# First attention of a two-layer block: loads of the stacked q and k walk the 8 features outermost instead of the 3 repeats

## The chip, the cores and the metric

The kernel runs on one core of a Trainium2 chip. The metric is the device time of one execution in microseconds (us). The profile comes from one execution of the same program.

## The reference, cut to what matters

The model is a block of two layers over an input of 16 batches of 128 rows and 256 columns. Its first step, and the only one that the change touches, is a cross attention with 16 heads of 8 features:

```
q = split_heads(einsum('bsf,of->bso', layernorm(x)^T, Wq) + bq)     # 16 heads, head size 8
k = split_heads(einsum('bsf,of->bso', ctx^T, Wk) + bk)
v = split_heads(einsum('bsf,of->bso', ctx^T, Wv) + bv)
attn = softmax(einsum('bhqd,bhkd->bhqk', q, k) / sqrt(128))         # 256 x 256 for each of 16 heads and 16 batches
out = einsum('bhqk,bhkd->bhqd', attn, v);  x = x + tanh(g) * (out Wo + bo)^T
```

After it come a layer of 64 experts, an mLSTM, and a second block with attention and four experts.

## The kernel before, in words

The code is written for the five engines one by one, with semaphores between them and every order fixed by hand.

The float32 q and k of the first attention are each split into three bf16 parts. A score needs all nine products of a part of q with a part of k, so nine blocks of 8 features are stacked on the contraction axis: 72 rows (`TERM_ROWS`) of 16 heads x 256 positions, 8 KB a row. Rows 72 to 74 (`MAX_ROWS`) hold the three parts of the negative row maximum against rows of ones in k, so that a second product gives the scores with the maximum already taken off. Tiles `qs` and `ks` hold one batch each, in a ring of four (`A_RING`).

- In a first stage (to about 70 us) q and k of all batches are computed, split and stored to DRAM as `a_q_parts` and `a_k_parts`, each [batch, 3 parts, 128, 256] in bf16 (`store_parts`, L161). Row p of the 128 is feature d = p // 16 of head p % 16, so that one feature of all heads is one contiguous run of 8 KB. ScalarE can write `parts` of pair i only when the stores of pair i - 3 have landed.
- `stack(b)` (L164) fills the tiles of batch b from DRAM with six DMAs of 192 KB. For t = 0, 1, 2 it loads rows 24t to 24t + 23: in `qs` three repeats of part t of q (L175), in `ks` the three parts of k once (L176). `stack(0)` is issued after the third `store_parts`; `stack(1)` to `stack(3)` after the last; then four loads of kept weights (below); and `stack(b + 4)` once the last exponentials' product of batch b is done.
- TensorE runs over heads: `score_max` (L262, 72 rows) puts the scores of a head in a bank and VectorE takes their maximum (L481), 28 heads ahead (`AHEAD`) of `exponentials` (L290, 75 rows), whose bank ScalarE turns into exponentials (L398); `times_v` (L304), `normalise` (L314), `to_features` (L323) and `residual` (L328) finish the batch. When a batch's 16 maxima are there, TensorE turns them into rows (L272), ScalarE and GpSimd split them in three (L385 to L536), and SyncE loads them into rows 72 to 74 of `qs` with three DMAs of 8 KB (`max_rows`, L204). `exponentials(b, 0)` waits for these three.
- Beside this, weights of the last block are split in two parts ("kept" work): at each `max_rows` SyncE stores the split of two units (L190, four DMAs of 256 KB) and loads two new ones (L184, two of 256 KB), which wait for those stores. GpSimd does the rounding.

All DMAs go through SyncE's one queue, so they are issued in this order: ..., `max_rows(b)`, stores, loads, `stack(b + 3)`, `max_rows(b + 1)`, ...

Of the kernel before, what the change touches and what calls it, by code (L numbers as in the profile page):

```python
# [23 lines left out]
DMA = 16  # L24
# [47 lines left out]
HEADS, HD = 16, 8  # L72
POS = D
# [34 lines left out]
def kept_units(k):  # L108

    io, units = k.io, []  # L110
    for h in range(RH):
        units.append((io["b_wqk"][h], [k.qk_parts[h, i] for i in range(2)]))
    for g in range(RH // GROUP):
        for half in range(2):
            cols = slice(half * KEPT, (half + 1) * KEPT)
            units.append((io["b_wv"][g][:, cols], [k.v_parts[g, i][:, cols] for i in range(2)]))
    for h in range(0, RH, 2):
        units.append((io["b_wo"][h:h + 2].rearrange("h p n -> p h n"), [k.o_parts[h:h + 2, i].rearrange("h p n -> p h n") for i in range(2)]))
    return units


def kept_places(k, u, shape):

    first = (u % KEPT_SLOTS) * 2 * KEPT
    whole, high = (k.columns[:, :, :].rearrange("p k t -> p (k t)")[:, at:at + KEPT] for at in (first, first + KEPT))
    return [t if len(shape) == 2 else t.rearrange("p (h n) -> p h n", h=shape[1]) for t in (whole, high)]


def kept_of(b):

    return range(KEPT_EACH * b, min(KEPT_EACH * (b + 1), 2 * RH))
# [9 lines left out]
def layer0_sp(k, m, s, ring):  # L141

    sp, io = k.nc.sync, k.io

    def load_inputs(chunk):
        b = slice(chunk * CHUNK, (chunk + 1) * CHUNK)
        sp.dma_start(k.resid[:, b, :], io["x"][b, :, :].rearrange("b p n -> p b n")).then_inc(k.x_in[chunk], DMA)
        sp.dma_start(k.ctx[:, b, :], io["ctx"][b, :, :].rearrange("b p n -> p b n")).then_inc(k.ctx_in[chunk], DMA)

    load_inputs(0)  # L150
    sp.dma_start(k.gates[:, :], io["gates"]).then_inc(k.gates_in, DMA)
    for dst, name in ((m.wqT, "a_wqT"), (m.wkT, "a_wkT"), (m.wvT, "a_wvT"), (m.woT, "a_woT"), (m.bias, "a_bias")):
        sp.dma_start(dst[:, :], io[name]).then_inc(s.weights_in, DMA)
    for chunk in range(1, NCHUNK):
        load_inputs(chunk)

    def store_parts(i):
        for n, (name, ready) in enumerate((("q", s.q_low), ("k", s.k_low))):
            sp.wait_ge(ready, i + 1)
            for j in range(2):  # L160
                sp.dma_start(io[f"a_{name}_parts"][2 * i + j].rearrange("t p n -> p t n"),  # L161
                             m.parts[i % A_SLOTS][:, n, :, j * POS:(j + 1) * POS]).then_inc(ring[f"{name}_out"][i % A_SLOTS], DMA)

    def stack(b):  # L164
        r, i = b % A_RING, b // 2
        flat = lambda t, first, count: t[first * HD:(first + count) * HD, :, :].rearrange("p h n -> p (h n)")
        parts_of = lambda n: io[f"a_{n}_parts"][b].rearrange("t (d h) n -> t d (h n)", d=HD)
        sp.wait_ge(ring["q_out"][i % A_SLOTS], 2 * DMA * (i // A_SLOTS + 1))
        sp.wait_ge(ring["k_out"][i % A_SLOTS], 2 * DMA * (i // A_SLOTS + 1))
        if b < A_RING:  # L170
            sp.wait_ge(s.k_ones, b + 1)
        else:
            sp.wait_ge(s.exp_scores, (b - A_RING + 1) * HEADS)
        for t in range(3):
            sp.dma_start(flat(m.qs[r], 3 * t, 3), parts_of("q")[t].unsqueeze(0).broadcast_to([3, HD, HEADS * POS])).then_inc(ring["stack_in"][r], DMA)  # L175
            sp.dma_start(flat(m.ks[r], 3 * t, 3), parts_of("k")).then_inc(ring["stack_in"][r], DMA)  # L176

    units = kept_units(k)

    def load_kept(u):  # L180
        r = u % KEPT_SLOTS
        if u >= KEPT_SLOTS:
            sp.wait_ge(ring["kept_out"][r], 2 * DMA * (u // KEPT_SLOTS))
        sp.dma_start(kept_places(k, u, units[u][0].shape)[0], units[u][0]).then_inc(ring["kept_in"][r], DMA)  # L184

    def store_kept(u):
        low, high = kept_places(k, u, units[u][0].shape)
        sp.wait_ge(s.kept_low, u + 1)
        for dst, src in zip(units[u][1], (high, low)):
            sp.dma_start(dst, src).then_inc(ring["kept_out"][u % KEPT_SLOTS], DMA)  # L190

    def kept(b):

        if b:
            for u in kept_of(b - 1):
                store_kept(u)
            for u in kept_of(b + 1):
                load_kept(u)

    def max_rows(b):  # L200
        sp.wait_ge(s.max_split, b + 1)
        for part in range(MAX_ROWS):
            row = TERM_ROWS + part
            sp.dma_start(m.qs[b % A_RING][row:row + 1, :, :].rearrange("o h (q n) -> o (h q) n", q=2),  # L204
                         m.mparts[b % 2][:, part, :]).then_inc(ring["max_in"][b % A_RING], DMA)
        kept(b)

    for i in range(1, NB // 2 + 1):
        store_parts(i - 1)
        if i == 3:  # L210
            stack(0)
    for b in range(1, A_RING):
        stack(b)
    for u in range(KEPT_SLOTS):
        load_kept(u)
    for i in range(AHEAD):
        if i >= 2 and (i - 2) % HEADS == HEADS - 1:
            max_rows((i - 2) // HEADS)
    for n in range(A_STEPS):
        for h in range(2):  # L220
            i = 2 * n + h + AHEAD - 2
            if i % HEADS == HEADS - 1 and i // HEADS < NB:
                max_rows(i // HEADS)
        if n % A_PAIRS == A_PAIRS - 1 and n // A_PAIRS + A_RING < NB:
            stack(n // A_PAIRS + A_RING)
    for u in kept_of(NB - 1):
        store_kept(u)
    for r in range(KEPT_SLOTS):
        sp.wait_ge(ring["kept_out"][r], 2 * DMA * (2 * RH // KEPT_SLOTS))
# [2084 lines left out]
```

## Time and profile before

| what | us |
|---|---|
| time, median of 3 runs | 1835.76 (1823.01 to 1838.44) |
| the profiled execution's own time | 1829.41 |
| its span in the trace | 1828.1 |
| first attention within it | about 0 to 391 |
| TensorE busy | 1633.9 (89%) |
| VectorE busy | 1103.7 (60%) |
| ScalarE busy | 1007.5 (55%) |
| GpSimd busy | 609.9 (33%) |

Busy time is the sum over the instructions of an engine. The chain of waits goes back from the last instruction, at each step to what released it. "PEclk" is the clock granted to TensorE, as a share of 2.4 GHz: 1.00 is 2.4 GHz and 0.50 is 1.2 GHz. In a list of instructions, [3.92 <-DMA x] means that the engine stood idle for 3.92 us before this one until DMA x landed. "SPq" stands for DMAs issued by SyncE: their time is that of the issue, not of the transfer.

### The profile page before, as it was taken

To read this page: it belongs to the slowest core of one execution; us is meant where nothing else is said; L and a number is where in the kernel's file an instruction comes from. 1 tells how busy PE (TensorE), PEld (TensorE's weight loads), DVE (VectorE), ACT (ScalarE), POOL (GpSimd) and SP (SyncE) were. 2 spreads that over 40 slices of the span, in tenths; PEclk is the share of its full clock that TensorE was granted. 3 is DMA by queue.
4 is the path that set the end of the run, shared out by engine and by line. 5 is a ranking of instruction groups with operands and counts; after the bars stand their busy time and mean duration, and the time that the engine had idled before them with its cause. 6 is when DMAs were issued, how large, how long until landed. Compare 5 with 4: busy or idle time off the path is not lost.

```text
span 1828.1 us, 30253 instructions
## 1 busy us (share of the span) xinstructions
PE 1633.9 (89%) x10996; PEld 1279.5 (70%) x10996; DVE 1103.7 (60%) x2052; ACT 1007.5 (55%) x2050; POOL 609.9 (33%) x495
## 2 busy tenths in 40 slices
PE   4368889878999999999998695899999999999898
PEld 2135455436888888888886342688888888888687
DVE  6456677637854445544446457676777777667454
ACT  4246667664443334433333664776777877776443
POOL 5222223212443533333332001454455455444000
PEclk9568888889999999999998787899999999999799
DMA  5634545335344334344330001435434334332310
GB/s 158 156 101 155 152 159 170 120 125 130 104 105 114 109 99 113 101 111 112 107 96 4 8 4 35 147 110 170 137 110 139 122 111 139 127 113 71 78 47 24
DMA packets 110980, 196.15 MB, mean 107 GB/s; under 512 B 16664, under 2 KB 59484, under 8 KB 108016
## 3 DMA queue, kind: packets, MB, share of 16 engines
q1 hardware_dynamic: 110832, 194.21, 35.9%
q8 instruction: 89, 1.46, 0.3%
q14 instruction: 59, 0.48, 0.1%
HBM read 167.64 MB, written 25.73 MB: 106 GB/s over the span
## 4 chain that ended last, share of the span: by engine, by line
PE 69%; DMA 8%; DVE 7%; ACT 5%; issue 5%; SPq 3%; POOL 3%; POOLq 0%; ACTq 0%; DVEq 0%
PE bank L67 16%; PE bank L69 16%; PE bank L68 16%; DMA a_qs<-a_mparts 6%; PE bank L1790 3%; PE bank L1758 3%; PE bank L304 2%; PE bank L290 2%; PE bank L262 2%; PE bank L1780 1%; POOL e_hidden L1008 1%; PE bank L1290 1%; PE bank L1289 1%; SPq L204 1%; PE bank L1300 1%
## 5 line engine op out<-in xcount | busy, mean ns | idle before, releaser
L1008 POOL TENSOR_TENSOR e_hidden<-e_gated,e_comb_wide 128x512 f32<-128x512 f32 x132 | 211.3, 1600 | 347.0 <-DVE e_gated L973 331.1
L848 ACT CAST e_hidden_hi<-e_hidden 128x512 fp32r<-128x512 f32 x132 | 82.0, 622 | 321.2 <-POOL e_hidden L1008 321.2
L481 DVE TENSOR_REDUCE a_negmax<-bank 128x2 f32<-128x512 f32 x256 | 166.7, 685 | 104.9 <-PE bank L262 103.5
L966 DVE TENSOR_TENSOR e_hidden_lo<-e_hidden,e_hidden_hi 128x512 fp32r<-128x512 f32 x132 | 98.2, 744 | 211.5 <-ACT e_hidden_hi L848 211.5
L69 PE MATMUL bank<-e_x_hi,e_weights_lo 128*128 128x512 f32 (+1 forms) x528 | 209.3, 396 | 0.0
L67 PE MATMUL bank<-e_x_hi,e_weights_hi 128*128 128x512 f32 (+1 forms) x528 | 208.4, 395 | 0.7 <-ACT e_comb_rows L808 0.7
L68 PE MATMUL bank<-e_x_lo,e_weights_hi 128*128 128x512 f32 (+1 forms) x528 | 208.3, 395 | 0.0
L1869 ACT ACTIVATE b_turned<-bank,b_swap_bias 64x512 f32<-64x512 f32 x256 | 174.9, 683 | 43.1 <-PE bank L69 39.3
L398 ACT ACTIVATE a_exp<-bank 128x512 f32<-128x512 f32 x256 | 144.3, 596 | 71.9 <-PE bank L290 66.0
L2018 POOL TENSOR_TENSOR b_turned<-b_turned,b_rope_q 128x512 f32<-128x512 f32 x64 | 82.8, 1294 | 258.8 <-ACT b_turned L1869 258.8
L69 PE MATMUL bank<-e_weights_hi,e_hidden_lo 128*128 128x256 f32 (+1 forms) x528 | 149.0, 282 | 0.0
L67 PE MATMUL bank<-e_weights_hi,e_hidden_hi 128*128 128x256 f32 (+1 forms) x528 | 147.8, 280 | 0.5 <-DVE e_hidden_lo L966 0.5
L68 PE MATMUL bank<-e_weights_lo,e_hidden_hi 128*128 128x256 f32 (+1 forms) x528 | 148.0, 280 | 0.0
L290 PE MATMUL bank<-a_qs,a_ks 75*128 75x256 bf16 x512 | 108.0, 298 | 41.1 <-DMA a_qs<-a_mparts 40.2
L262 PE MATMUL bank<-a_ks,a_qs 72*128 72x256 bf16 x512 | 114.5, 312 | 33.0 <-DMA a_ks<-a_k_parts 13.7
L1968 DVE TENSOR_TENSOR b_straight<-b_straight,b_turned 128x512 f32<-128x512 f32 x128 | 141.2, 1141 | 0.0
L973 DVE TENSOR_TENSOR e_gated<-e_silu,bank 128x512 f32<-128x512 f32 x132 | 90.5, 686 | 56.6 <-PE bank L69 44.1
L1935 DVE SCALAR_TENSOR_TENSOR b_straight<-bank,b_head_bias,b_rope_q 128x512 f32<-128x512 f32 x64 | 48.0, 749 | 111.2 <-ACT b_turned L1869 111.1
L69 PEld LDWEIGHTS bank<-e_x_hi,e_weights_lo 128*128 128x128 f32 (+1 forms) x528 | 98.7, 187 | 22.8
L67 PEld LDWEIGHTS bank<-e_x_hi,e_weights_hi 128*128 128x128 f32 (+1 forms) x528 | 99.2, 188 | 19.7 <-ACT e_comb_rows L808 1.1
L68 PEld LDWEIGHTS bank<-e_x_lo,e_weights_hi 128*128 128x128 f32 (+1 forms) x528 | 98.7, 187 | 18.8
L67 PE MATMUL bank<-b_x_hi,b_qk_hi 128*128 128x512 f32 x256 | 102.5, 401 | 4.8 <-DVE b_x_lo L1927 3.4
(327 smaller groups left out, 4156.6 us busy)
## 6 DMA issues: line engine op xcount, KB each, us to landing
e_comb_wide<-e_combT SPq DMA_DIRECT2D x130, 256.0 KB, 4.0
e_raw<-in_e_weights SPq DMA_DIRECT2D x64, 384.0 KB, 4.6
b_qk_hi<-b_qk_parts SPq DMA_DIRECT2D x64, 256.0 KB, 2.7
b_qk_lo<-b_qk_parts SPq DMA_DIRECT2D x64, 256.0 KB, 3.0
a_qs<-a_q_parts SPq DMA_DIRECT2D x48, 192.0 KB
a_ks<-a_k_parts SPq DMA_DIRECT2D x48, 192.0 KB
b_qk_parts<-columns SPq DMA_DIRECT2D x32, 256.0 KB, 3.6
b_vw_hi<-b_v_parts SPq DMA_DIRECT2D x16, 512.0 KB, 3.9
```

Of the source, the lines that this page charges most:

```text
L67: pe.matmul(out, w_hi, x_hi, start=start, stop=False, skip_group_check=True)
L68: pe.matmul(out, w_hi, x_lo, start=False, stop=False, skip_group_check=True)
L69: return pe.matmul(out, w_lo, x_hi, start=False, stop=stop, skip_group_check=True)
L262: last = pe.matmul(bank[:, qb * POS:(qb + 1) * POS], m.qs[r][0:TERM_ROWS, h, qb * P:(qb + 1) * P], m.ks[r][0:TERM_ROWS, h, :], start=True, ...
L290: last = pe.matmul(bank[:, kb * POS:(kb + 1) * POS], m.ks[r][0:ROWS, h, kb * P:(kb + 1) * P], m.qs[r][0:ROWS, h, :], start=True, stop=True)
L398: act.activation(m.expo[at % A_EXPS][:, :, :].rearrange("p k q -> p (k q)"), banks[2 + h % 2][:, :], ACT.Exp, scale=float(1 / np.sqrt(np.f ...
L481: dve.tensor_reduce(m.negmax[b % 2][:, h, :], banks[h % 2][:, :].rearrange("p (q n) -> p q n", q=2), AX.X, ALU.max, negate=True).then_inc( ...
L966: dve.tensor_tensor(lo[0:rows, :], m.hidden[at % 2][0:rows, :], hi[0:rows, :].bitcast(F32), ALU.subtract).then_inc(s.hidden_lo)
L973: dve.tensor_tensor(m.gated[i][0:rows, :], m.silu[i][0:rows, :], banks[2 * i + 1][0:rows, :], ALU.mult).then_inc(s.gated)
L1008: pool.tensor_tensor(m.hidden[i][0:rows, :], m.gated[i][0:rows, :], m.comb_wide[u % E_RING][0:rows, chunk * BANK:(chunk + 1) * BANK], ALU. ...
L1869: last = act.activation(w.turned[i][dst:dst + half, which, :], banks[bank][src:src + half, :], ACT.Identity, bias=m.swap_bias[dst:dst + ha ...
L1968: dve.tensor_tensor(w.straight[n % 2][:, which, :], w.straight[n % 2][:, which, :], w.turned[n % 2][:, which, :], ALU.add).then_inc(s.rotated)
```

## The change

Both access patterns of the source change their outermost dimension. Before, a load of q walks 3 repeats (step 0), then 8 features, and one of k walks 3 parts, then 8 features. After, both walk 8 features first, and inside each the 3 repeats or the 3 parts. The destination, 24 rows of 8 KB, is the same, so row 24t + 8r + d of before becomes row 24t + 3d + r in both tiles; the products of a score are the same, added in another order. The bytes moved, the number of DMAs, their order in the queue and all waits stay.

```diff
     def stack(b):
         r, i = b % A_RING, b // 2
         flat = lambda t, first, count: t[first * HD:(first + count) * HD, :, :].rearrange("p h n -> p (h n)")
-        parts_of = lambda n: io[f"a_{n}_parts"][b].rearrange("t (d h) n -> t d (h n)", d=HD)
+        parts_of = lambda n: io[f"a_{n}_parts"][b].rearrange("t (d h) n -> d t (h n)", d=HD)
...
         for t in range(3):
-            sp.dma_start(flat(m.qs[r], 3 * t, 3), parts_of("q")[t].unsqueeze(0).broadcast_to([3, HD, HEADS * POS])).then_inc(ring["stack_in"][r], DMA)
+            sp.dma_start(flat(m.qs[r], 3 * t, 3), parts_of("q")[:, t:t + 1].broadcast_to([HD, 3, HEADS * POS])).then_inc(ring["stack_in"][r], DMA)
             sp.dma_start(flat(m.ks[r], 3 * t, 3), parts_of("k")).then_inc(ring["stack_in"][r], DMA)
```

## Rows read from the trace of the kernel before

**Rows 1.** The page: shares of the chain that ended last, by engine

```profile
PE 69%; DMA 8%; DVE 7%; ACT 5%; issue 5%; SPq 3%; POOL 3%; POOLq 0%; ACTq 0%; DVEq 0%
```

**Rows 2.** Chain in order of time, 40 to 400 us: start, us, what

```profile
46.09 11.69 DMA a_q_parts<-a_parts
...
100.96 13.33 DMA a_qs<-a_mparts
...
243.67 10.17 DMA a_qs<-a_mparts
...
315.45 10.26 DMA a_qs<-a_mparts
```

**Rows 3.** Waits of PE, 60 to 395 us: total, times, longest

```profile
PE bank L290 <- DMA a_qs<-a_mparts: 40.2, 12, 13.4
...
PE bank L262 <- DMA a_ks<-a_k_parts: 13.7, 1, 13.7
```

**Rows 4.** Busy time by stretch; DMA share is of 16 engines

```profile
core 0: us, PE busy (x) PEld busy (x) DVE busy (x) ACT busy (x) POOL busy (x), PEclk, DMA share, GB/s
102.00:108.00 6.00, 0.00 (x0) 0.00 (x0) 0.00 (x0) 0.00 (x0) 0.00 (x0) 0.50 0.20 80
250.00:252.00 2.00, 0.00 (x0) 0.00 (x0) 1.05 (x4) 0.13 (x1) 0.00 (x0) 0.84 0.19 78
187.00:191.00 4.00, 4.00 (x42) 2.38 (x40) 3.38 (x8) 3.44 (x10) 2.18 (x5) 1.00 0.69 150
74.00:84.00 10.00, 3.75 (x13) 0.77 (x12) 4.73 (x8) 0.00 (x0) 0.00 (x0) 0.50 0.73 144
133.29:365.35 232.06, 205.14 (x1831) 117.53 (x1829) 155.63 (x325) 151.20 (x313) 61.84 (x91) 0.85 0.49 151
217.60:227.60 10.00, 9.23 (x58) 4.49 (x59) 3.85 (x7) 4.37 (x9) 1.53 (x4) 0.51 0.51 129
230.85:244.63 13.78, 13.78 (x145) 8.28 (x142) 11.78 (x25) 11.54 (x24) 3.68 (x8) 1.00 0.56 169
```

**Rows 5.** DMA issues of SyncE in order of time, one batch

```profile
238.33 0.77 SPq L175 DMA_DIRECT2D a_qs<-a_q_parts  x1
...
242.43 1.84 SPq L204 DMA_DIRECT2D a_qs<-a_mparts  x3
244.31 2.12 SPq L190 DMA_DIRECT2D b_qk_parts<-columns  x4
```

**Rows 6.** TensorE in order of time: one clean batch, then a wait

```profile
225.75 1.86 PE L304 MATMUL bank<-a_exp,a_vaug 128*9 128x256 f32 x16
...
230.85 0.44 PE L323 MATMUL bank<-ident,a_outq 128*128 128x128 f32 x2
...
240.34 1.05 PE L304 MATMUL bank<-a_exp,a_vaug 128*9 128x256 f32 x16
...
244.63 0.44 PE L323 MATMUL bank<-ident,a_outq 128*128 128x128 f32 x2
...
253.89 0.61 PE L290 MATMUL bank<-a_qs,a_ks 75*128 75x256 bf16 x2 [3.92 <-DMA a_qs<-a_mparts]
```

**Rows 7.** TensorE, transposes of the maxima, batches 2 and 15

```profile
133.29 0.28 PE L272 MATMUL bank<-ident,a_negmax 128*32 128x128 f32 x1
...
365.35 0.28 PE L272 MATMUL bank<-ident,a_negmax 128*32 128x128 f32 x1
```

**Rows 8.** SyncE issues, 68 to 98 us

```profile
70.94 0.71 SPq L175 DMA_DIRECT2D a_qs<-a_q_parts  x1
...
83.09 3.54 SPq L176 DMA_DIRECT2D a_ks<-a_k_parts  x1
86.69 10.99 SPq L184 DMA_DIRECT2D columns<-in_b_wqk  x4
```

**Rows 9.** Issues that fill q and k stacks, L175 and L176: ns min/median/max

```profile
L175 SPq DMA_DIRECT2D a_qs<-a_q_parts x48: 697/746/2021, 41.5 to 330.9; - x48
...
L176 SPq DMA_DIRECT2D a_ks<-a_k_parts x48: 403/445/3545, 42.4 to 331.6; - x48
```

**Rows 10.** Loads of the maxima (L204), from issue to landing

```profile
DMA to landing us min/median/max: 1.8/2.9/13.3
```

## The prediction, written before the changed kernel was run

> **What bounds the kernel now.** I first read the shares of the chain that ended last: TensorE has 69%, but a DMA share of 8% stands beside it [rows 1], some 146 us of 1828, and the change is about DMAs. The chain in order of time shows where they lie. In the first attention it goes again and again through one transfer, the load of the maxima into rows 72 to 74 of `qs`, with 10.17 and 10.26 us from issue to landing for 8 KB; the first takes 13.33 us; and earlier there is one of 11.69 us, a store of q parts [rows 2]. Alone, such a load of maxima takes as little as 1.8 us [rows 10]. So it isn't its own size that makes it late, but what lies ahead of it on the DMA engines. TensorE stands still for it 40.2 us in 12 waits, and once 13.7 us for a stack [rows 3].
>
> What lies ahead is seen in the DMA share by stretch. Just before a wait ends, the share is 0.19 to 0.20 of 16 engines at 78 to 80 GB/s, in two stretches 150 us apart [rows 4]: that is 3 engines at some 26 GB/s each, and 13 empty ones. Nothing but stack loads runs there, and 3 is the outermost count of the q load. Earlier in a stack the share is 0.69 to 0.73 at 144 to 150 GB/s [rows 4], 11 or 12 engines. I read this so: a k load is spread over 12 engines, a q load over 3, and engines 0 to 2 carry both. A q load is 24 rows of 8 KB, 196.6 KB, so three take 590 KB / 78 GB/s = 7.6 us; the k loads another 590 KB / 150 = 3.9 us; together 11.5 us. The case of one batch agrees: the stack's issue begins at 238.33, the maxima are issued from 242.43 [rows 5] and land at 243.67 + 10.17 = 253.84 [rows 2], 15.5 us after the stack began, and TensorE goes on at 253.89 after 3.92 us of idling [rows 6].
>
> The wait costs twice. After it the granted clock is at 0.51 for 10 us [rows 4], the lower of the two levels, 1.2 GHz, and a `times_v` group takes 1.86 us in place of 1.05 at 2.4 GHz [rows 6].
>
> **The change, part by part.**
>
> *Spread of the loads.* The outermost count of both sources becomes 8. I take 8 engines for all six loads, at 26 GB/s each 208 GB/s: 1.18 MB a stack in 5.7 us. The other bound is the rate at which 11 or 12 engines did these loads, 150 GB/s, which is no better per engine than 13: 7.9 us. I take 7.5, nearer to the measured rate of the same rows. Against 11.5 to 12 now.
>
> The Trainium skill, DMA: Bandwidth & Descriptors, in the section on why a DMA increments its semaphore by 16, says that a DMA uses the largest number of engines up to 16 that divides the outermost sizes of both sides; for 3 against 24 rows that is 3, for 8 against 24 it is 8, and the rows with 3 engines agree. The same rule speaks against half of the change: the k loads lose engines (12 to 8). The SBUF page (SBUF — State Buffer, Door 1) says that 24 neighbouring partitions reach only 6 of 16 ports of 27.2 GB/s; an estimate from it is 163 GB/s whatever the number of engines, so 7.2 us a stack, and k would lose nothing. The 144 to 150 GB/s of 12 engines agree with such a ceiling.
>
> *The 13 batches in the middle.* From the maxima's transpose of batch 2 (133.29) to that of batch 15 (365.35) [rows 7] there are 13 periods in 232.06 us, 17.85 each, with a mean clock of 0.85 [rows 4]. One without a wait and at full clock lasted 244.63 - 230.85 = 13.78 us, with TensorE busy for all of it [rows 6, 4]; it is the price of a batch when TensorE is the bound. Is the wait gone? In the case above the stack begins at 238.33, late, since SyncE's loads of kept weights ahead of it wait for stores that themselves lie behind the last stack. The transfer starts at about 239.1, ends 7.5 us later at 246.6, and the maxima, in the queue since 244.3 [rows 5], land some 1.5 us after, at about 248. TensorE needs them at 253.89 - 3.92 = 249.97 [rows 6]. With 7.9 us it is still 1.6 us in time. And since the stores ahead also land sooner, the next stack is issued sooner. So I take all waits as gone: 13 x (17.85 - 13.78) = 52.9 us, of which the idle time itself is 40.2 - 13.4 = 26.8 us [rows 3] and the rest lower clock. Lower bound: some waits of a microsecond stay and keep the clock down now and then; with half of the periods clean it is 30 us. Upper bound 55.
>
> *The start.* The store of q parts at 46.09 lands at 57.78 [rows 2], behind `stack(0)`, whose issue begins at 41.5 [rows 9]. With transfers from 42.5 to 50, store and landing come at about 52: 5.5 us earlier (3 to 7). Then `stack(1)` to `stack(3)` are issued from 70.94 on [rows 8], now 65.4. The 18 loads take 22.5 us from 66.2, so to 88.7; the four kept loads behind them, 1 MB, have half on the same eight engines, 0.52 MB / 208 GB/s = 2.5 us; the first maxima follow with 1.5: 92.7 to 93.2. Before, they landed at 100.96 + 13.33 = 114.3 [rows 2]. That is 21 us with the 5.5 in it. TensorE's wait of 13.7 us for the second stack [rows 3] mostly goes inside this: the stack lands at some 75, and the maxima are computed well before 93. At 5.7 us a stack the start gives 27 us, at 9 it gives 16.
>
> *What it costs.* The k load has one dimension more, as the q load has now: its issue may take 0.75 us in place of 0.45 [rows 9], 0.9 us a stack. Behind it in SyncE's queue stand the maxima of the next batch; 0.9 us fits in the 1.6 to 2 us left above. Before the first maxima it is 9 x 0.3 = 2.7 us, covered by transfers that run until 88.7, while the issues of SyncE that now take 3.54 and 10.99 us [rows 8] should shorten. Without that cover it would cost 2.7 us. The order of rows costs TensorE nothing: same shapes, same number. Everything behind 391 us is untouched.
>
> **Sum.** 52.9 + 21 = 74 us off the profiled execution's 1829.4: 1755. The median of the runs shown lies 6.4 us above that execution, so the same sum gives 1762 there. I forecast 1758, between the two.
>
> **Rivals.**
>
> *The stack gains half or less.* Eight engines on few partitions could get in each other's way: a stack takes 10 to 11 us. For it: 12 engines did no better than 150 GB/s. Against: 3 did 78. Then a stack started at 238.3 lets the maxima land at about 251, a wait of 1 us in many batches with the clock down after each; I put 2 us a period, 26 us, and 8 us at the start: 1802.
>
> *The number of engines doesn't change*, or the maxima wait for something else as long, such as the rounding work's stores and loads: 1834. Against it: the share falls to 3/16 exactly where only q loads are left.
>
> *Slower: the repeats of one row now lie on one engine.* Each engine reads the same 8 KB three times in a row and writes three neighbouring partitions, and engines 0 to 7 are all behind one another. Should a row take over 12.4 / 18 = 0.69 us on each of the 8 engines, a stack takes longer than now. At 0.8 us it is 14.4 us, the maxima come 2 us later than now in each batch, and the start loses 3 x 2.5 us minus what overlaps: 13 x 1.7 + 4 = 26 us, 1861. Against it: 12 engines at 150 GB/s took 12 x 8.2 KB / 150 = 0.66 us a row, and 3 engines 0.31; 8 should lie between.
>
> *All engines at full rate*: 5.7 us a stack, nothing waits: 27 + 55 = 82 us, 1747.
>
> **How the numbers follow.** Forecast, with its own bounds of 1747 to 1790: 0.80, the full-rate case in it. Half gain, 1802: 0.10. No change, 1834: 0.06. Slower, 1861: 0.04. The range 1745 to 1797 takes in the bounds (16 + 30 = 46 us off 1836 is 1790) and an edge of the half-gain case. Of this kernel a measurement can tell about 1% from no change, 18 us. Faster by over 1% is the forecast and nearly all of the half-gain case: 0.90. Within 1%: 0.06. Slower: 0.04.
>
> **What would show it.** In the profile after: no stretch of 0.19 share with 78 GB/s; instead 0.5 while a stack runs, at 150 to 208 GB/s. Waits of TensorE for the load of maxima: one, at the start, under 13 us, and none later. Transposes of the maxima 13.8 us apart, and a clock near 1.00 from the second batch to the last. The issue of a k load at 0.75 us. The first maxima landing at about 93. The prediction is wrong if the share stays at 3/16, if a stack takes over 10 us, or if at 13.8 us a period something else comes due, the kept loads on SyncE or VectorE, which is busy 11.78 of 13.78 us [rows 4].

## The result, and the profile after

The changed kernel takes 1759.3 us, median of 4 runs (1755.62 to 1764.16), against 1835.2 before, now the median of 4 runs too: ratio 0.960, 95% interval 0.955 to 0.965. Five rounds later gave 1761.3 us and 0.964 (0.961 to 0.967). The forecast was 1758. The profiled execution took 1760.46 us, 68.95 less than the one before.

The page first: its span and the shares of the chain by engine.

```profile
span 1759.2 us, 30253 instructions
...
PE 78%; DVE 7%; ACT 5%; issue 4%; DMA 2%; POOL 2%; SPq 1%; ACTq 0%; POOLq 0%; DVEq 0%
```

DMA has gone from 8% of the chain [rows 1] to 2%. In order of time only two long DMA pieces are left in the first attention, the store of q parts and the first load of maxima. The second is no shorter than before (14.49 us, 13.33 in [rows 2]); it begins 18.8 us sooner.

```profile
46.34 6.43 DMA a_q_parts<-a_parts
...
82.14 14.49 DMA a_qs<-a_mparts
```

The load of the maxima stops TensorE once, where it was 12 times and 40.2 us [rows 3]:

```profile
PE bank L290 <- DMA a_qs<-a_mparts: 11.3, 1, 11.3
```

The busy time by stretch (the two columns at the end are the DMA share of 16 engines and GB/s):

```profile
core 0: us, PE busy (x) PEld busy (x) DVE busy (x) ACT busy (x) POOL busy (x), PEclk, DMA share, GB/s
86.00:90.00 4.00, 0.00 (x0) 0.00 (x0) 0.13 (x1) 0.00 (x0) 0.00 (x0) 0.50 0.51 150
72.00:78.00 6.00, 2.70 (x11) 0.97 (x11) 2.93 (x6) 0.35 (x2) 0.00 (x0) 0.50 0.51 158
187.00:191.00 4.00, 4.00 (x41) 2.54 (x40) 3.26 (x7) 3.49 (x8) 3.25 (x4) 1.00 0.69 233
115.58:294.00 178.42, 178.39 (x1830) 107.19 (x1827) 152.38 (x324) 149.46 (x312) 61.86 (x91) 1.00 0.61 196
```

The stretches at 0.19 [rows 4] are gone. While nothing but stack loads runs, the share is 0.51, so 8 engines, at 150 to 158 GB/s. In the middle (last row) the clock stays at 1.00, 2.4 GHz, and TensorE is busy for all of 178 us.

SyncE in one batch, to be held against [rows 5]:

```profile
180.91 0.72 SPq L175 DMA_DIRECT2D a_qs<-a_q_parts  x1
...
186.63 1.82 SPq L204 DMA_DIRECT2D a_qs<-a_mparts  x3
188.49 2.08 SPq L190 DMA_DIRECT2D b_qk_parts<-columns  x4
```

The stack's loads begin 5.7 us before the maxima are issued, 4.1 before. TensorE: the wait for stack 1, the wait for the first maxima, and the transposes of the maxima of batches 2 and 15, which answer to [rows 7]:

```profile
76.36 1.04 PE L262 MATMUL bank<-a_ks,a_qs 72*128 72x256 bf16 x4 [3.05 <-DMA a_ks<-a_k_parts]
...
96.67 0.61 PE L290 MATMUL bank<-a_qs,a_ks 75*128 75x256 bf16 x2 [11.34 <-DMA a_qs<-a_mparts]
...
115.58 0.27 PE L272 MATMUL bank<-ident,a_negmax 128*32 128x128 f32 x1
```

```profile
294.46 0.28 PE L272 MATMUL bank<-ident,a_negmax 128*32 128x128 f32 x1
```

Between the last two lie 178.88 us, 13.76 a batch against 17.85 before, so 53.2 us come from here: 26.8 of idle time [rows 3] and 26.4 from the clock. The first maxima release TensorE at 96.67 in place of 114.3, 17.7 us sooner. Together 70.9; what follows batch 15 took 2.0 us longer (1464.7 against 1462.8 us), which is within what two executions differ by. At the start SyncE now issues the stacks without being held up, unlike [rows 8], with the kept loads and the first maxima right behind:

```profile
65.94 0.68 SPq L175 DMA_DIRECT2D a_qs<-a_q_parts  x1
...
78.65 2.17 SPq L184 DMA_DIRECT2D columns<-in_b_wqk  x4
80.87 1.86 SPq L204 DMA_DIRECT2D a_qs<-a_mparts  x3
```

And an issue takes the same time for q and k, where it was 746 and 445 ns [rows 9]:

```profile
L175 SPq DMA_DIRECT2D a_qs<-a_q_parts x48: 653/654/820, 41.5 to 267.9; - x48
```

```profile
L176 SPq DMA_DIRECT2D a_ks<-a_k_parts x48: 653/654/702, 42.3 to 268.6; - x48
```

### The profile page after: what moved, and what is told of

It is laid out like the page before. It is cut to its first block, busy times and chain, and to the rows that moved or that the text cites. A ratio compares the mean times of both kernels' runs of the same rounds, so it can differ in the third digit from the quotient of the medians.

```text
span 1759.2 us, 30253 instructions
## 1 busy us (share of the span) xinstructions
PE 1610.3 (92%) x10996; PEld 1269.9 (72%) x10996; DVE 1101.2 (63%) x2052; ACT 1007.2 (57%) x2050; POOL 609.9 (35%) x495
## 4 chain that ended last, share of the span: by engine, by line
PE 78%; DVE 7%; ACT 5%; issue 4%; DMA 2%; POOL 2%; SPq 1%; ACTq 0%; POOLq 0%; DVEq 0%
PE bank L67 17%; PE bank L69 17%; PE bank L68 17%; PE bank L262 4%; PE bank L304 4%; PE bank L290 3%; PE bank L1790 3%; PE bank L1758 3%; PE bank L1780 1%; POOL e_hidden L1008 1%; PE bank L1290 1%; PE bank L1289 1%; PE bank L1300 1%; PE bank L1309 1%; PE bank L1754 1%
## 5 line engine op out<-in xcount | busy, mean ns | idle before, releaser
L262 PE MATMUL bank<-a_ks,a_qs 72*128 72x256 bf16 x512 | 106.5, 293 | 16.1 <-ACT a_parts L370 6.9
L290 PE MATMUL bank<-a_qs,a_ks 75*128 75x256 bf16 x512 | 98.4, 275 | 12.2 <-DMA a_qs<-a_mparts 11.3
```

What stands on the lines that cost most here:

```text
L262: last = pe.matmul(bank[:, qb * POS:(qb + 1) * POS], m.qs[r][0:TERM_ROWS, h, qb * P:(qb + 1) * P], m.ks[r][0:TERM_ROWS, h, :], start=True, ...
L290: last = pe.matmul(bank[:, kb * POS:(kb + 1) * POS], m.ks[r][0:ROWS, h, kb * P:(kb + 1) * P], m.qs[r][0:ROWS, h, :], start=True, stop=True)
```

## The experiments

Times are medians; each ratio is to the kernel before, on the same chip. Three kernels, q alone, k alone and q alone on spread rows, leave the right pairing of features: their rows of q and k meet other features, so that they compute other scores, at the same cost.

### Only q, or only k

```diff
         parts_of = lambda n: io[f"a_{n}_parts"][b].rearrange("t (d h) n -> t d (h n)", d=HD)
+        by_feature = lambda n: io[f"a_{n}_parts"][b].rearrange("t (d h) n -> d t (h n)", d=HD)
```

The kernel with q alone takes `by_feature` for the q load, as the change does, that with k alone for the k load; the other load keeps `parts_of`.

Expected of q alone: 

> Only the q loads walk the features outermost; the k loads are those of before, so the rows of the two tiles no longer pair the same features and the scores are other sums of the same size: its time is what counts. Theory of the busiest engine (a load runs on as many engines as its outermost count lets it, and the engine with most rows sets when a stack is through): q 9 rows on each of 8 engines, k 6 on each of 12, so 15 rows on the busiest against 30 before and 18 in the changed kernel. Expected 1755 to 1762 us, no wait for the maxima after the first. Rival (the gain lies in the k loads, or takes both together): 1800 to 1836.

Expected of k alone: 

> Only the k loads walk the features outermost, q as before; again the rows pair otherwise, and its time is what counts. Busiest engine: 24 q rows and 9 k rows on engines 0 to 2, 33 against 30 before: no gain, 1836 to 1855 us, with DMA share down to 3 of 16 before each landing of maxima. Rival (k carries the gain): 1760 to 1800.

Measured: q alone 1783.0 us, ratio 0.976 (0.972 to 0.980); k alone 1839.2, 1.007 (1.004 to 1.010). The waits of TensorE for the maxima after the start, first k alone (12 waits), then q alone:

```profile
PE bank L291 <- DMA a_qs<-a_mparts: 32.2, 12, 5.4
```

```profile
PE bank L291 <- DMA a_qs<-a_mparts: 15.3, 8, 4.0
```

K alone is as the theory of the busiest engine had it: three engines keep all of q, and in the stretches before its waits end the share is 0.16 to 0.21. Q alone keeps some two thirds of the gain, but it should have been the best of all by the count of rows, 15 on the busiest engine against 18 in the changed kernel. It missed by over 20 us. (Its profiled execution took 1796.4 us, the longest of its four, so its waits are rather more than usual.) Its windows show where: while loads on 8 and on 12 engines run together there are stretches, these are the slowest, in which 12 engines are busy and move 94 to 106 GB/s, 8 to 9 GB/s each.

```profile
200.00:204.00 4.00, 4.00 (x47) 2.17 (x40) 3.25 (x7) 3.09 (x7) 3.67 (x7) 1.00 0.78 94
184.00:186.00 2.00, 2.00 (x23) 1.56 (x15) 1.29 (x3) 1.67 (x4) 1.33 (x2) 1.00 0.77 106
```

So the number of rows on the busiest engine isn't all; in such a stretch a row's price rises from 0.31 to about 1 us. The change of k, which takes four engines from the k loads, brings some 22 to 29 us beside that of q (ratio 0.976 against the changed kernel's 0.964 and 0.960) and costs 11 us alone (1828.6 to 1839.2).

### Four engines or eight, same rows, same places

Both kernels cut each load of the changed kernel in two, so that 12 loads fill a stack. One cuts by features (outermost count 4):

```diff
+            for half in range(2):
+                rows, d = slice(24 * t + 12 * half, 24 * t + 12 * half + 12), slice(4 * half, 4 * half + 4)
+                sp.dma_start(m.qs[r][rows].rearrange("p h n -> p (h n)"), parts_of("q")[d, t:t + 1].broadcast_to([4, 3, HEADS * POS])).then_inc(ring["stack_in"][r], DMA)
+                sp.dma_start(m.ks[r][rows].rearrange("p h n -> p (h n)"), parts_of("k")[d]).then_inc(ring["stack_in"][r], DMA)
```

The other cuts by columns (outermost count 8), and the k load in the same way:

```diff
+            for half in range(2):
+                cols = slice(half * HEADS * POS // 2, (half + 1) * HEADS * POS // 2)
+                sp.dma_start(flat(m.qs[r], 3 * t, 3)[:, cols], parts_of("q")[:, t:t + 1, cols].broadcast_to([HD, 3, HEADS * POS // 2])).then_inc(ring["stack_in"][r], DMA)
```

Expected of the cut by features: 

> Same rows in the same places and the same walk as in the changed kernel, but each load is cut in two by features, so that its outermost count is 4 and 12 loads fill a stack. Busiest engine: 36 rows on each of 4 engines, at 0.31 us a row 11.3 us a stack, about what 30 rows at mixed rates took before: waits for the maxima in most batches, DMA share 0.25 at about 105 GB/s in a stack, 1810 to 1850 us. Rival (what helped is that the repeats of a row lie together in source and tile): 1760 to 1770, like the changed kernel.

Expected of the cut by columns: 

> The control to the cut by features: each load is cut in two by columns, 12 loads of the same size, outermost count still 8. Busiest engine: 18 rows in 36 halves, 7 to 8 us a stack; the issues take 12 x 0.65 = 7.8 us of each batch's 13.8 on SyncE, and 5 us more before the first maxima. Expected 1760 to 1772 us. If the number of loads is what costs in the cut by features, this one is as slow as that.

Measured: by features 1854.7 us, 1.014 (1.011 to 1.016); by columns 1780.2, 0.976 (0.971 to 0.980). By features the time lies just over the 1810 to 1850 that I expected. The share is 0.24 to 0.25, four engines, and the waits are back. They move 84 GB/s in a stretch of the middle, and 96, 24 each, at the start where stack loads run alone for 18 us; I had expected 105. Waits first:

```profile
PE bank L292 <- DMA a_qs<-a_mparts: 40.1, 12, 5.0
```

```profile
174.00:181.00 7.00, 7.00 (x73) 4.35 (x72) 5.57 (x13) 6.00 (x14) 4.46 (x7) 0.99 0.24 84
76.00:94.00 18.00, 8.09 (x29) 2.14 (x29) 8.52 (x15) 1.70 (x3) 1.11 (x3) 0.50 0.25 96
```

The same walk of the source with the same rows side by side gains nothing once 4 engines do it. So the order of rows and repeats by itself brings nothing, and the number of engines is shown to be a cause. Each load of the cut by features also goes to 12 neighbouring rows and not 24. That this is the cause instead isn't likely: at 24 GB/s each of the four engines ran near the 26 of the three engines before. The number of loads has a price too, which I had put at under 13 us and is about 21: in the cut by columns SyncE issues 12 loads in 8.5 us, and the next maxima stand behind them.

```profile
147.13 0.73 SPq L177 DMA_DIRECT2D a_qs<-a_q_parts  x1
...
154.91 0.65 SPq L178 DMA_DIRECT2D a_ks<-a_k_parts  x1
155.60 1.82 SPq L206 DMA_DIRECT2D a_qs<-a_mparts  x3
157.46 2.05 SPq L192 DMA_DIRECT2D b_qk_parts<-columns  x4
160.45 3.64 SPq L186 DMA_DIRECT2D columns<-in_b_wqk  x2
```

The maxima are issued at 155.60 to 157.42, and TensorE, due at 157.5, waits for their landing:

```profile
159.39 0.60 PE L292 MATMUL bank<-a_qs,a_ks 75*128 75x256 bf16 x2 [1.89 <-DMA a_qs<-a_mparts]
```

The transfers are fast enough here; it is the queue of SyncE that is late. In the profile this makes 8 waits of 11.7 us in all in the middle, and the first maxima release TensorE at 100.92, 4.3 us after the changed kernel. The long issue at 160.45 is its wait for the stores of kept weights.

### Crowded rows

Three experiments on the price of a row. In the first, load t fills every third row of the tile in place of 24 neighbours (q in the same way as k here):

```diff
-        flat = lambda t, first, count: t[first * HD:(first + count) * HD, :, :].rearrange("p h n -> p (h n)")
+        every_third = lambda t, first: t[first:TERM_ROWS:3, :, :].rearrange("p h n -> p (h n)")
...
-            sp.dma_start(flat(m.ks[r], 3 * t, 3), parts_of("k")).then_inc(ring["stack_in"][r], DMA)
+            sp.dma_start(every_third(m.ks[r], t), parts_of("k")).then_inc(ring["stack_in"][r], DMA)
```

Expected: 

> Six loads on 8 engines as in the changed kernel, from the same source walk, but load t fills every third row of the tile (rows t, t + 3, ... t + 69), so that the 24 rows of a load are spread over 72 partitions and one engine's three rows are no neighbours. In the changed kernel a row took 0.37 to 0.44 us with 8 engines on 24 neighbouring rows, 150 to 156 GB/s, against 0.31 us with 3 engines. Theory of crowded partitions (The Trainium skill, page SBUF — State Buffer, Door 1: 24 neighbouring partitions reach 6 ports, 72 reach 10; an estimate from its table): near 200 GB/s, 5.9 us a stack in place of 7.5, nothing gained in the middle, 4 to 6 us at the start: 1753 to 1757. Rival (the source side or the engines in pairs limit the rate): 150 GB/s stays, 1757 to 1762.

The second is the kernel before with its q loads cut into three of 8 neighbours:

```diff
-            sp.dma_start(flat(m.qs[r], 3 * t, 3), parts_of("q")[t].unsqueeze(0).broadcast_to([3, HD, HEADS * POS])).then_inc(ring["stack_in"][r], DMA)
+            for repeat in range(3):
+                sp.dma_start(flat(m.qs[r], 3 * t + repeat, 1), parts_of("q")[t]).then_inc(ring["stack_in"][r], DMA)
```

Expected: 

> The kernel before, row order and k loads unchanged, but each q load is cut into its three repeats, of 8 rows each: outermost count 8 with no change of order. If only the number of engines matters, 15 rows on the busiest and 1760 to 1785, as with q alone changed. If neighbouring rows crowd each other, 8 neighbours at a time are the worst case: with 12 neighbours per 80 GB/s (6 rows in step 1, 24 at 150 GB/s) a load of 65 KB takes 1.0 to 1.3 us, nine of them 9 to 12 us beside the k loads, and the maxima wait as before: 1810 to 1840.

Measured: every third row 1752.2 us, 0.958 (0.954 to 0.963); 8 neighbours 1814.1, 0.992 (0.989 to 0.996). With every third row the same 8 engines (share 0.51) move 202 GB/s, and the first maxima release TensorE at 91.47, 5.2 us before the changed kernel. The time itself, 0.958 against 0.960 and 0.964, isn't told apart from the changed kernel's:

```profile
70.00:78.00 8.00, 5.20 (x19) 1.50 (x19) 5.59 (x10) 1.70 (x3) 1.11 (x3) 0.50 0.51 202
```

```profile
74.88 1.04 PE L262 MATMUL bank<-a_ks,a_qs 72*128 72x256 bf16 x4 [2.18 <-DMA a_ks<-a_k_parts]
...
91.47 0.61 PE L290 MATMUL bank<-a_qs,a_ks 75*128 75x256 bf16 x2 [7.62 <-DMA a_qs<-a_mparts]
```

With 8 neighbours, and k on 12 engines beside them, it is 125 GB/s at a share of 0.72. So eight engines for q bring under 1% here; the run has 12 loads and the mix of 8 and 12 engines too, so it puts no price on the 8 neighbours alone.

```profile
196.00:200.00 4.00, 4.00 (x29) 1.78 (x27) 1.62 (x4) 1.99 (x6) 1.95 (x5) 0.53 0.72 125
```

A third run puts the case of q alone on spread rows, which tells the crowding from the mere mix of 8 and 12 engines:

Expected: 

> The case of q alone changed (q loads on 8 engines, k loads on 12, rows pairing other features, so only its time counts) with load t filling every third row. With 24 neighbouring rows this mix took 0.6 to 1.3 us a row and 1783 us, slower than 8 and 8 engines, against the rule of the busiest engine. If the crowding of neighbouring rows did that, the spread rows undo it: 1748 to 1760 us and no waits in the middle. If it is the mix of 8 and 12 engines itself, 1770 to 1790 with waits in the middle.

Measured: 1750.7 us, 0.958 (0.955 to 0.961), with no wait in the middle; 194 GB/s at a share of 0.68 at the start. At 0.68, 11 engines, k is still on more than 8. In the same stretch of its time q alone has nearly the same share and moves 115 GB/s (second line); the mix costs nothing when the rows lie apart.

```profile
70.00:76.00 6.00, 3.16 (x13) 0.99 (x13) 3.39 (x6) 0.71 (x3) 0.23 (x1) 0.50 0.68 194
70.00:76.00 6.00, 5.05 (x18) 1.03 (x16) 5.59 (x10) 0.00 (x0) 0.00 (x0) 0.50 0.69 115
```

```profile
73.99 1.03 PE L263 MATMUL bank<-a_ks,a_qs 72*128 72x256 bf16 x4 [2.51 <-DMA a_ks<-a_k_parts]
...
90.95 0.61 PE L291 MATMUL bank<-a_qs,a_ks 75*128 75x256 bf16 x2 [7.99 <-DMA a_qs<-a_mparts]
```

Destination rows that lie side by side are what made rows dear in q alone: the two kernels differ in nothing else. That each load reaches few ports of the memory, as the Trainium skill has it (SBUF — State Buffer, Door 1: 6 ports of 27.2 GB/s for 24 neighbours, 163 GB/s as an estimate), fits the 150 to 158 GB/s of the changed kernel; for every third row its table gives 10 ports, and 8 engines reached 202. The 94 GB/s of the mix are far under that ceiling, and no run here shows why.

### The order at the start

```diff
-    for b in range(1, A_RING):
+    for b in range(1, A_RING - 1):
         stack(b)
-    for u in range(KEPT_SLOTS):
-        load_kept(u)
     for i in range(AHEAD):
         if i >= 2 and (i - 2) % HEADS == HEADS - 1:
             max_rows((i - 2) // HEADS)
+    for u in range(KEPT_SLOTS):
+        load_kept(u)
+    stack(A_RING - 1)
```

Expected on the changed kernel: 

> The changed kernel with another order on SyncE at the start: stacks 1 and 2, then the first maxima, then the four kept loads, then stack 3. In the changed kernel the first maxima were issued at 80.9 behind stacks 2 and 3 and the kept loads, and landed at 96.6, TensorE idle for 11.3 us before. Expected: behind stack 2 alone they land at 84 to 86, 11 us of idling gone, stack 3 in time (needed some 19 us later): 1746 to 1750. Rival (the order at the start only moves the wait to stack 3 or to the kept rounding): 1757 to 1762.

Expected on the kernel before: 

> The same reordering in the kernel before. If what lies ahead in the rings of engines 0 to 2 is the wait, the first maxima land one stack (11 to 12 us) and the kept loads (2 to 4 us) sooner, at about 100 in place of 114, and the middle stays with its waits: 12 to 15 us under before, 1815 to 1820. Rival (the first maxima wait for something else): 1828.

Measured: on the changed kernel 1742.6 us, 0.954 (0.950 to 0.959); on the one before 1820.6, 0.995 (0.992 to 0.998). On the changed kernel the wait for the first maxima is gone: they are issued at 78.42, and TensorE goes from `score_max` into the exponentials without one (the last of the `score_max` before them is at 83.72, the first exponentials' product at 84.12, 12.5 us before that of the changed kernel). By the ratios this order brings 11 to 17 us; I had expected 9 to 13. The profiled execution took 1756.0 us, the other three 1741 to 1743; in its middle it has four short waits for the maxima, of 0.36 to 1.03 us, 3.0 in all, and its clock stays at 1.00.

```profile
78.42 1.85 SPq L204 DMA_DIRECT2D a_qs<-a_mparts  x3
80.32 2.00 SPq L184 DMA_DIRECT2D columns<-in_b_wqk  x4
```

```profile
75.36 1.04 PE L263 MATMUL bank<-a_ks,a_qs 72*128 72x256 bf16 x4 [2.60 <-DMA a_ks<-a_k_parts]
...
83.72 0.61 PE L263 MATMUL bank<-a_ks,a_qs 72*128 72x256 bf16 x2 [0.18 <-DVE a_negmax L482]
```

On the kernel before TensorE is released at 106.23, 8.1 us sooner and not the 14 that I expected (at about 100); the time falls by 6 us, at the edge of my 1815 to 1820. Stack 1 is late as before (90.45 against 91.97), and the middle keeps its waits.

```profile
90.45 1.03 PE L263 MATMUL bank<-a_ks,a_qs 72*128 72x256 bf16 x4 [11.51 <-DMA a_ks<-a_k_parts]
...
106.23 0.61 PE L291 MATMUL bank<-a_qs,a_ks 75*128 75x256 bf16 x2 [6.82 <-DMA a_qs<-a_mparts]
```

Last, the order with every third row, beside the changed kernel on one chip:

Expected of the changed kernel again: 

> The changed kernel once more, beside the two below on one chip: 1755 to 1762 us. The ratio to before again 0.955 to 0.965.

Expected of both together: 

> Every third row for each load and the new order at the start together. The order alone took out the wait for the first maxima, and what is left there is a wait of 2.6 us for stack 1 and one of 1.03 us in the middle of its profile; rows loaded at 0.32 to 0.35 us in place of 0.41 shorten stack 1 by some 1.5 us. Expected 1740 to 1746 us, ratio to the changed kernel 0.99. If the spread rows and the order gained the same microseconds, no better than the order alone (1742 to 1747); if they added up in full, 1735.

Measured: the changed kernel 1761.3 us, 0.964 (0.961 to 0.967); both together 1748.8, 0.956 (0.953 to 0.958). By these ratios it beats the changed kernel by 0.8%; it isn't told apart from the order alone, and the 1740 to 1746 that I expected were too low. The only DMA that TensorE waits for in its stacks is the second one at the start:

```profile
PE bank L263 <- DMA a_ks<-a_k_parts: 1.7, 1, 1.7
```

## Why the prediction was right

- *Three engines for q, and eight after.* Right. The share before a landing went from 0.19 to 0.51, k alone (q left on three) gained nothing, and four engines brought all the waits back.
- *The middle.* Forecast 52.9 us, measured 53.2. All waits went at once, and with them the lower clock, which was half of the sum. (Half of the forecast 52.9 is 26.5 and not the 30 that stands there as the lower bound; with it the bound is 1793, still inside the range.)
- *The start.* Forecast 21, measured 17.7. The store of q parts landed at 52.77, 5.0 us sooner (5.5 forecast). Then the term was mis-sized by the rate of the 18 loads. I let them run from 66.2 at 157 GB/s, 7.5 us a stack, to 88.7. In the trace their rows, packets of 8 KB, run from 67.4 to 92.4: 142 GB/s, 8.3 us a stack, over the 7.9 that I had as the bound. They were slowest at 80 to 86, while half of the kept loads ran beside them. The other half came behind, and the 4 us that I gave it and the maxima were right: landing at 96.6 in place of 93. In stretches with stack loads alone it was 150 to 158 GB/s, 7.5 to 7.9 us a stack.
- *The issue of a k load.* Forecast 0.75 us, measured 0.654, while that of q fell by 0.09: a stack's issue grew by 0.35 us and not 0.9. The cover named for it held. The cut by columns shows how thin it was: 4 us more of issue per stack costs about 21 us.
- *K loses engines.* Half right. The prediction held this half of the change to be a loss or nothing. Alone it is a loss of 11 us. But the runs show that q alone would have brought 1783, since 8 and 12 engines on neighbouring rows slow each other down; beside the change of q, giving k the same 8 was part of the gain.
- *The rivals.* The half gain (a stack of 10 to 11 us) is what q alone shows; the slower one (rows over 0.69 us) what happens in it for some stretches. Four engines give nearly the time of the slower one, 1854.7 in place of 1861, by another cause: 36 rows on each at about 0.34 us. Neither came with 8 and 8. The 12.4 us behind the 0.69 stand in no row; with the prediction's own 11.5 to 12 us a stack it would be 0.64 to 0.67.
- *Luck.* For the profiled execution the sum gave 1755, and it took 1760.5: 3.3 us are the start, 2.0 lie behind batch 15. The forecast came within 1.3 us of the median because it stood between this sum and one 6.4 us higher.

## What to carry to other kernels

Look at the DMA share just before a wait on a small transfer ends: 0.19 with nothing else running is three engines with a queue and thirteen without, and the outermost count of the access pattern is the first suspect. A load of 8 KB that takes 10 us is late for what stands ahead of it, so ask both which transfers could be spread wider and which could be issued after it. When loads go to few neighbouring partitions, spread the rows of each load over the tile: it cost nothing here and gave 202 GB/s in place of 150 to 158, though the gain in time was too small to be told from noise.

## What the runs showed of the hardware that was not expected

- Loads on 8 and on 12 engines into neighbouring rows: 94 to 106 GB/s in all in the slowest stretches, with 12 engines busy, and 115 over the 6 us at 70 to 76. The same mix with rows three apart, at 70 to 76: 194 GB/s.
- The same 8 engines with the same source: 150 to 158 GB/s into 24 neighbouring rows, 202 into every third of 72.
- Four engines into 12 neighbours did 84 to 96 GB/s, 21 to 24 each, where three in the kernel before did 78 to 80, 26 each.
- SyncE's issue of a load took 445 ns for k's contiguous source, 654 for the two patterns with 8 outermost, 746 for 3 repeats outermost. It isn't the pattern alone: the same k load took 293 ns where the q loads ahead of it were of 8 rows each.
